# Experts of ten of thirteen tiles run on rows sorted by expert, with indirect DMAs, in a decoder layer on one core

## What is computed

```
gates = softmax(einsum('bsh,eh->bse', x, gate_w) + gate_b)      # 8 experts
top_gates, top_idx = lax.top_k(gates, 2)
expert_out = einsum('bsh,eoh->bseo', x, expert_w) + expert_b
selected = take_along_axis(expert_out, top_idx[..., None], axis=2)
return (selected * top_gates[..., None]).sum(axis=2)
```

## Time and profile before

| | |
|---|---|
| median of the runs | 1438.62 us |
| profiled execution, its own time | 1441.02 us |
| its span, first to last instruction | 1439.2 us |
| granted TensorE clock, mean over the span | 0.969 |
| busy: TensorE, DVE, POOL, ACT | 93%, 63%, 48%, 43% |
| DMA, mean | 35 GB/s |
| start of iteration 15, of iteration 16's first work | 1043.5, 1109.5 us |
| experts behind all chunks, until the last tile's matmuls | 1145.5 to 1435.8 us |

### The profile page before, as it was taken

One profiled execution on the slowest core, in us unless ns is written; L12 is line 12 of the kernel. 1 busy time (PEld: TensorE's weight loads), 2 busy tenths in 40 slices (PEclk: granted clock), 3 DMA queues, 4 the chain that ended last, 5 costly groups with the idle time before them and its releaser, 6 DMA issues.

```text
span 1439.2 us, 43985 instructions
## 1 busy us (share of the span) xinstructions
PE 1341.8 (93%) x19700; PEld 856.9 (60%) x19700; DVE 901.2 (63%) x1463; ACT 614.7 (43%) x888; POOL 684.5 (48%) x642
## 2 busy tenths in 40 slices
PE   4689999999999999999999999999956799999999
PEld 4365766667576666757676675767644444444444
DVE  4657777686777768677776867777563443333332
ACT  4236555555655555564555556455534010000000
POOL 1435757666575666657576665757555100000000
PEclk9899999999999999999999999999967699999999
DMA  7011010101101010110101011010201100101002
GB/s 269 1 39 32 9 44 3 45 8 40 38 8 45 2 45 8 39 38 8 45 3 44 8 40 37 10 45 3 82 31 37 54 30 4 35 36 36 8 0 92
DMA packets 27538, 50.37 MB, mean 35 GB/s; under 512 B 1612, under 2 KB 13188, under 8 KB 27356
## 3 DMA queue, kind: packets, MB, share of 16 engines
q1 hardware_dynamic: 27356, 47.62, 10.2%
HBM read 41.06 MB, written 6.55 MB: 33 GB/s over the span
## 4 chain that ended last, share of the span: by engine, by line
PE 85%; DVE 7%; POOL 3%; ACT 2%; issue 1%; DMA 1%; SPq 0%; POOLq 0%; ACTq 0%; DVEq 0%
PE psum L254 58%; PE psum L664 7%; PE psum L753 6%; PE psum L738 4%; DVE c_most L986 2%; PE psum L682 2%; PE psum L641 2%; DVE c_max L991 2%; PE psum L633 1%; DMA arena<-in_L_attn_Wv 1%; PE psum L345 1%; PE psum L366 1%; POOL arena L1157 1%; PE psum L597 1%; PE psum L649 1%
## 5 line engine op out<-in xcount | busy, mean ns | idle before, releaser
L1157 POOL TENSOR_TENSOR arena<-prob,arena 128x1200 f16<-128x1200 f32 x128 | 314.3, 2467 | 188.3 <-ACT arena L847 188.3
L986 DVE TENSOR_REDUCE c_most<-psum 100x4 f32<-100x1444 f32 x128 | 211.5, 1652 | 21.0 <-PE psum L738 18.8
L254 PE MATMUL psum<-w_kv,cT 128*128 128x512 f16 (+1 forms) x864 | 199.7, 379 | 0.5
L254 PE MATMUL psum<-cT,w_kv 128*128 128x361 f16 x1152 | 196.4, 322 | 0.0
L477 DVE SCALAR_TENSOR_TENSOR w_self_all<-psum,g_now,w_self_all 128x512 f32<-128x512 f32 x104 | 77.8, 750 | 168.6 <-PE psum L254 168.6
L838 ACT ACTIVATE prob<-psum 128x1200 f32<-128x1200 f32 x128 | 149.8, 1170 | 70.5 <-PE psum L753 56.6
L847 ACT ACTIVATE arena<-prob 128x1200 f16<-128x1200 f32 x128 | 151.3, 1196 | 1.5
L254 PEld LDWEIGHTS psum<-cT,w_kv 128*128 128x128 f16 x1152 | 106.0, 99 | 65.2 <-issue 4.0
L254 PEld LDWEIGHTS psum<-w_kv,cT 128*128 128x128 f16 (+1 forms) x864 | 83.4, 101 | 90.6 <-DVE c_raw L901 5.1
L954 DVE SCALAR_TENSOR_TENSOR arena<-psum,b_part,arena 128x361 f16<-128x361 f32 x128 | 74.3, 591 | 86.1 <-ACT arena L819 86.1
L829 ACT ACTIVATE cv<-psum 128x512 f16<-128x512 f32 x96 | 57.3, 597 | 163.0 <-PE psum L254 163.0
(11 more groups left out here) (179 smaller groups left out, 2175.6 us busy)
## 6 DMA issues: line engine op xcount, KB each, us to landing
c_raw<-in_ctx SPq DMA_DIRECT2D x16, 960.0 KB
cT<-in_L_ffn_expert_w SPq DMA_DIRECT2D x4, 1024.0 KB, 5.2
cv<-in_L_ffn_expert_w SPq DMA_DIRECT2D x4, 1024.0 KB, 5.3
x_in<-in_x SPq DMA_DIRECT2D x16, 200.0 KB
x_scratch<-x_out SPq DMA_DIRECT2D x16, 200.0 KB
w_self_all<-x_scratch SPq DMA_DIRECT2D x12, 256.0 KB, 4.4
out<-w_self_all SPq DMA_DIRECT2D x12, 256.0 KB, 2.0
c_raw<-in_ctx SPq DMA_DIRECT2D x16, 123.0 KB
```

Of the source, the lines that this page charges most:

```text
L254: last = pe.matmul(out_ap, a(pa), b(pb), start=(i == 0 and j == 0), stop=(i == len(pairs) - 1 and j == 2))
L986: dve.tensor_reduce(c_most[:, hf], score[0:L, :, 0:HC], AXIS.X, ALU.max).then_inc(max_done, 1)
L1157: pool.tensor_tensor(prob16[o % 2][:, (2 + part) * PT:(3 + part) * PT], prob[:, part], prob16[o % 2][:, part * PT:(part + 1) * PT], ALU.su ...
```

## The change

- The weights of all eight experts are turned in iteration 15, two chunks FW per step from step 5 on (the last two in iteration 16), into one tensor `wT_all` that lies over the weights of attention. SP loads the raw weights of expert e + 2 as soon as expert e is turned.
- The ten early tiles keep a buffer each, and their norm is made in place. Logits get a chunk for each tile.
- Routing of the ten tiles moves to iteration 15, step 15. A new chunk FR computes, for every row, its place among the rows of its expert (11 small matmuls with a triangle and with ones), and DVE derives two slots for every row and the expert of each of 27 slot tiles (`dve_place`, 19 operations with the copy that releases the bank).
- POOL scatters the normed rows into `xs_dram`, 27 x 128 slots, with 20 indirect DMAs (10 tiles, 2 picks) in iteration 16. The slots were set to zero in iteration 1 by a DMA of 27 x 256 KB.
- The experts' stage: 6 dense tiles (experts 0 and 1 on the last three), 27 slot tiles, 18 dense tiles (experts 2 to 7 on the last three), 51 tiles for 104. A slot tile is loaded, turned in fp32, split, multiplied with the weights of the expert whose number TensorE reads into a register, evicted by ACT and stored to `ys_dram`. None is computed ahead of the gate `ALL_CHUNKS`.
- POOL gathers for each row its two results (20 indirect DMAs, four buffers), DVE adds bias, residual and the two parts times their gates, beside the last dense tiles.

```diff
-ROUTE_STEP = 14
+ROUTE_STEP = 15
+SLOT_TILES = 2 * EARLY + E - 1
+SLOTS = SLOT_TILES * P
+DENSE_FIRST = 2
 EXTRA_CHUNKS = {
-    B - 1: {4: ["FX0"], 5: ["FG0", "FW0", "FX1"], 6: ["FW1", "FX2"], 7: ["FW2", "FW3", "FX3"],
-            **{t + 4: [f"FX{t}"] for t in range(4, EARLY)}, LAST_STEP: ["FL0"]},
+    B - 1: {h: ([f"FG0"] if h == 2 else []) + ([f"FX{h - 4}"] if 0 <= h - 4 < EARLY else []) +
+            ([f"FL{h - 5}"] if 0 <= h - 5 < EARLY else []) + (["FR"] if h == ROUTE_STEP + 1 else []) +
+            [f"FW{i // KD}{i % KD}" for i in (2 * h - 10, 2 * h - 9) if 0 <= i] for h in range(2, LAST_STEP + 1)},
...
+        ORDER = ([("dense", e, t) for e in range(DENSE_FIRST) for t in range(EARLY, TT)] +
+                 [("slots", j, None) for j in range(SLOT_TILES)] +
+                 [("dense", e, t) for e in range(DENSE_FIRST, E) for t in range(EARLY, TT)])
+        AHEAD = 2
...
         def ffn_sync(sp):
             sp.wait_ge(chunk_out, ALL_CHUNKS)
+            sp.wait_ge(scattered, 16 * 2 * EARLY)
+            for j in range(4):
+                load_slots(sp, j)
+            for j in range(SLOT_TILES):
+                sp.wait_ge(slot_out, j + 1)
+                sp.dma_start(ys_dram[j * P:(j + 1) * P], slots_out[:, j % 4]).then_inc(slots_stored[j % 4], 16)
+                if j + 4 < SLOT_TILES:
+                    sp.wait_ge(slotsT_low, j + 1)
+                    load_slots(sp, j + 4)
...
+            for i, (kind, a, t) in enumerate(ORDER):
+                if turned_at(i) is not None:
+                    turn_slots(turned_at(i))
+                if i >= 4:
+                    if ORDER[i - 4][0] == "dense":
+                        pe.wait_ge(y_done, dense_count(i - 4))
+                    else:
+                        pe.wait_ge(slot_out, ORDER[i - 4][1] + 1)
...
+                    pe.wait_ge(slotsT_low, a + 1)
+                    e = pe.value_load(expert_i[0:1, a:a + 1], min_val=0, max_val=E - 1)
+                    split3(pe, bank_out, [(lambda p, k=k: slotsT[a % 3][:, p, k],
+                                           lambda p, k=k: wT_all[:, bass.ds(e, 1), k, p].rearrange("p e f -> p (e f)"))
+                                          for k in range(KD)]).then_inc(slot_ready, 1)
...
+        def pool_scatter(pool, t):
+
+            if t == 0:
+                pool.wait_ge(placed, 1)
+                pool.wait_ge(slots_zeroed, 16)
+            for i in range(2):
+                pool.indirect_dma_start(xs_dram[:, :], bass.IndirectOffsetOnAxis(ap=slot_i[:, i, t:t + 1], axis=0),
+                                        y_norm[t], None).then_inc(scattered, 16)
+
+        def ffn_pool(pool):
+            for i in range(4):
+                pool.wait_ge(slots_stored[i], 16 * ((SLOT_TILES - i + 3) // 4))
+            pool.wait_ge(chunk_out, ALL_CHUNKS)
+            for t in range(EARLY):
+                if t >= 4:
+                    pool.wait_ge(sum_done, t - 3)
+                for i in range(2):
+                    pool.indirect_dma_start(part[i][:, t % 4], None, ys_dram[:, :],
+                                            bass.IndirectOffsetOnAxis(ap=slot_i[:, i, t:t + 1], axis=0))\
+                        .then_inc(parts_loaded[t], 16)
...
         def ffn_norm(pool, it, t):
...
-            if t >= 2:
-                before = it if f"FX{t - 2}" in it.order else its[B - 1]
-                pool.wait_ge(chunk_out, before.done(f"FX{t - 2}"))
+            if t >= EARLY + 2:
+                pool.wait_ge(chunk_out, it.done(f"FX{t - 2}"))
...
                 if n == B and h == LAST_STEP:
+                    for t in range(EARLY):
+                        pool_scatter(pool, t)
                     for t in range(EARLY, TT):
                         ffn_norm(pool, it, t)
```

More of the change, by code:

```diff
@@ new lines, in build_layer, with dense_count, turned_at, bias_at @@
+        AHEAD = 2
+        PLACE_CONSTS = 8
+        def dense_count(i):
+            return sum(o[0] == "dense" for o in ORDER[:i + 1])
+        def turned_at(i):
+            return ORDER[i + AHEAD][1] if i + AHEAD < len(ORDER) and ORDER[i + AHEAD][0] == "slots" else None
+        GATES_AT = DENSE_FIRST * LATE + 4
+        BIAS_FROM = len(ORDER) - (E - DENSE_FIRST) * LATE
+        BIAS_ORDER = tuple(range(EARLY, TT)) + tuple(range(EARLY))
+        def bias_at(i):
+            n = i - BIAS_FROM
+            return n if 0 <= n < TT else None
@@ L321, in ffn_sync, with store_sum, load_slots @@
+        def store_sum(sp, t):
+            sp.wait_ge(sum_done, t + 1)
+            sp.dma_start(out.rearrange("b l d -> (b l) d")[t * P:(t + 1) * P], part_sum[:, t % 4])\
+              .then_inc(sum_stored[t % 4], 16)
+        def load_slots(sp, j):
+            sp.dma_start(slots[:, j % 4], xs_dram[j * P:(j + 1) * P]).then_inc(slots_loaded[j % 4], 16)
         def ffn_sync(sp):
             sp.wait_ge(chunk_out, ALL_CHUNKS)
-            def next_raw(e, odd, pair, more):
-                if isinstance(e, int) and e == 0:
-                    load_expert(sp, 2, 0)
-                elif not isinstance(e, int) or e < E - 2:
-                    sp.wait_ge(e_low, KD * e)
-                    load_expert(sp, e + 2, odd)
@@ L330, in ffn_sync @@
-            experts(sp, next_raw)
-            for t in range(TT):
-                n = min(P, T - t * P)
-                sp.wait_ge(y_done, TT * (E - 1) + t + 1)
-                sp.dma_start(out.rearrange("b l d -> (b l) d")[t * P:t * P + n], y[0:n, t]).then_inc(y_stored, 16)
-            sp.wait_ge(y_stored, 16 * TT)
-        def pe_expert_T(pe, e, odd, pair, k):
-            c = KD * (e - 1) + k
-            if k == 0:
-                pe.wait_ge(e_loaded[odd], 16 * (pair + 1))
-            if not (isinstance(c, int) and c < 2):
-                pe.wait_ge(e_low, c - 1)
-            for o in range(KD):
-                last = pe.transpose(psum[:, 4 + k % 2, o * P:(o + 1) * P], raw_e[odd][:, o, k * P:(k + 1) * P], ident[:])
-            last.then_inc(e_T, 1)
@@ L545, in sync_iteration @@
                 sp.dma_start(x2_dram[n - 1], x_out[:]).then_inc(x2_stored, 16)
[L546 to L550 removed]
+            if n == B:
+                for t in range(EARLY, TT):
+                    load_y(sp, t)
             if n < B - 2:
@@ L760, in pe_iteration @@
             for h, step in enumerate(it.steps):
-                if it.n == B and h == LAST_STEP:
-                    pe.wait_ge(chunk_out, it.all_before())
-                    for t in range(AHEAD):
-                        pe_tile(pe, 0, 0, t)
                 for name in step:
@@ L965, in dve_chunk @@
             elif kind == "FL":
[L966 to L970 removed]
+                op = dve.scalar_tensor_tensor(gates[:, i], f[:, 0:E], 1.0 / WSCALE, g_bias[:], ALU.mult, ALU.add)
+            elif kind == "FR":
+                dve_place(dve, f[:, 0:(EARLY + 1) * E].rearrange("p (t e) -> p t e", e=E))
+                dve.wait_ge(placed, 1)
+                op = dve.tensor_copy(best[:, 0:1], slot_f[:, 0, 0:1])
             elif kind == "CV":
```

448 lines of the change are left out of this document (289 added, 159 removed).

## The result

The median is 1364.28 us (1362.64 to 1367.44, four runs) against 1437.17 us of the kernel before on the same chip (1434.79 to 1440.55, four runs): a ratio of 0.9489 [0.9466, 0.9511], 5.1% faster. The forecast was 1345 (1311 to 1385): the direction is right, the time lies inside the range, and the forecast is 19 us too low. The profiled execution took 1362.64 us with a span of 1360.9. The changed kernel was timed once more beside later experiments: 1367.23 us, ratio 0.9503 [0.9481, 0.9524]. The brackets behind a ratio are its 95% interval.

What follows compares the result with a forecast made beforehand. TensorE, busy 93% of the span, bounds the kernel, except iteration 15 (a DVE, ACT and POOL chain). Of 149 us saved, 11 go for early tiles, 17 gate, 12 turning slots, 19 late loads, the rest in transitions: 1345 us (1311 to 1385).

Steps and rivals of the forecast that it cites:

- rival that ends slower: Scatters and gathers: POOL held through each indirect DMA, reaching 1439 at 4.2 us each, about 1469 at 5.0; chance 4%.
- Slots: 27 slot tiles: late loads make 3.77 us per tile, 3.85 with the register load; 100.7 us for the tiles.
- The second rival: Slot tiles: the register load drains TensorE, 15 to 33 us more, 1360 to 1378; chance 14%.
- Half clock in the slots: Slot tiles: waits of 0.8 us per tile keep TensorE at 1.2 GHz, 164 us for 101, time 1408; chance 8%.
- Scatter: POOL in iteration 16: 20 indirect DMAs at 1.2 us, 24 us in all, ahead of the norms of tiles 10 to 12.
- Iteration 15, net +8: Iteration 15 gets 8 us longer from turning weights, routing and placement, less POOL's waits; bounds -11 to +31.
- Routing and placement, 4.5 + 2.5: Iteration 15: routing adds 4.5 us to the chain, placement, behind PV1's 2.8 us of matmuls, 2.5.
- The chunks FW, 9.5: Iteration 15: about half of 19.3 us of evictions for 26 more chunks and the logits is not covered, 9.5 us.
- POOL's waits, -8.5: Iteration 15: POOL no longer waits for FX chunks before reusing two y_norm buffers, which gives 8.5 us back.
- Zeroing, "nothing": Iteration 1: zeroing 27 x 256 KB beside some 60 us of matmuls, on DMA engines 15% busy, costs nothing.
- Dense tiles with biases: End of the experts' stage: 18 tiles at 2.59 and 13 biases at 0.96 take 59.1 us.
- Gate: Before the experts: norms and logits keep their 10 us and the experts' gate opens at 1162.5, 17 us later.

Runs made afterwards that it cites:

- Experiment 1: Changed kernel with SP loading slot tile j + 4 before it waits for tile j's result and stores it: 1345.33 us, ratio 0.9367.
- Experiment 7: Experiment 1 with a fixed expert's weights for each slot tile, no register load or arithmetic: 1344.94 us, ratio 0.9344.
- the four profiles: Profiles of the changed kernel (twice), Experiment 1 and Experiment 7, identical up to the slots; 124.17 to 128.69 us from batch 13's store to batch 15's.
- Experiment 5: Changed kernel with routing at step 17 and chunk FR at step 18 of iteration 15, not 15 and 16: 1358.13 us, ratio 0.9442.
- Experiment 6: Changed kernel with 16 of 32 chunks FW, experts 4 to 7 using the weights of 0 to 3: 1351.26 us, ratio 0.9388.
- experiment 8: Changed kernel with the old wait put back, POOL's norm of tile t waiting for chunk FX of tile t - 2: 1368.54 us, ratio 0.9514.
- experiment 2: Changed kernel with SP issuing expert 4's load before it waits for and stores batch 14 in iteration 15: 1362.03 us, ratio 0.9477.
- experiment 3: Changed kernel with slots zeroed by nine DMAs in iterations 1 to 9, not one in iteration 1: 1357.27 us, ratio 0.9459.

## Why the prediction came out as it did

**The direction and the main saving: right.** 53 tiles fewer against some 37 us given back in waits is what the page shows, and no rival that ends slower came near: an indirect DMA held POOL for 1.27 us, not 4.2.

**Slots: right in the total and in the loop, with luck in the terms.** The forecast had 3.77 us per tile from a loop over two tiles, 3.85 with the register; the trace has 3.76. The forecast's lap was 4.5 us from one tile's matmuls to the next turning and 3.03 of turning and matmuls. The trace has 3.9 and 3.63 (7.52 together): the load landed sooner than taken, and behind each wait the turning, the gap and the matmuls take 0.6 us more. The two misses cancel, which is luck. Experiment 1 takes 18.7 us off the stage, where the sum had 19 for late loads. Of the register load the forecast said that it is hidden unless TensorE waits for a load, and took 0.08 per tile. Experiment 7 against experiment 1 shows both halves: nothing where TensorE runs on, 0.41 us behind a wait. In the changed kernel 0.20 of gap and 0.17 on the matmuls in each lap are near 0.19 per tile. The second rival, 1 to 2 us in every tile, falls. The Trainium skill's floor of about 600 ns for a register load ("DMA: Bandwidth & Descriptors", "Latency and other measured facts") does not hold here: the trace has 0.30 us for the median of 27 such loads and 0.55 for the longest.

**Half clock in the slots: wrong as a rival.** The granted clock was 0.50 before the gate and rose in the first tiles behind it (12.31 us for four, against 10.36 in the earlier trace rows). From 1188 us on it was 1.00, though 14 us of waits are spread over the slots.

**Scatter: right, in size partly by luck.** 1.27 us each for 1.2; 1.6 us more over the twenty. POOL is not held until the data land, as the forecast took it, but the rows only bounded the price between 0.43 and 2.7, and 1.2 was a choice between them. **Gather: right.** 0.95 us on POOL plus 0.30 (median landings 4.0 and 4.4), and DVE never waited for the rows; on the contrary POOL waited for DVE to free the buffers.

**Iteration 15, net +8: the step that was off, by 2.4 to 6.9 us** in the four profiles (+10.4 to +14.9; the table's profile has the most). Four of its terms were mis-sized or missing.

- Routing and placement, 4.5 + 2.5. They stand on the chain whole, 7.9 + 4.5 us. Placement was to hide behind PV1's 2.8 us of matmuls; that overlap was not there, since PV1's matmuls started only behind placement's last copy, after a wait of 4.00 us. Routing was to take 5.7 us, less 1.2 hidden; nothing of it was hidden, and one of its small operations took 2.37 us in place of 0.24 (last section). Experiment 5 gets 4 to 7 us back by moving routing.
- The chunks FW, 9.5 for half of their evictions and the logits'. On the chain of the four profiles the evictions on ACT and DVE have 7 to 8 us, so that half was about right. The turnings on TensorE, 11 to 24 us more in the forecast's own count, were given no term in the net sum, and 6 to 10 us of them are on the chain. Experiment 6 prices a whole chunk at 0.52 to 0.64 us, 14 to 17 for the 26.
- POOL's waits, -8.5. Before, the chain of iteration 15 does pass through POOL (12.4 of its 66 us), and in the changed kernel through none of it, so the waits were rightly read as a path. What they were worth was not: put back alone they cost 1 to 4 us (experiment 8), since other work is nearly as late behind them.
- The expert's load behind SP's wait for batch 14 was missing from the sum, about 2 us (experiment 2).

These single prices add to more than was measured, so they overlap: relief in one place is partly taken by the next. How they share the difference stays open.

**Zeroing, "nothing": wrong.** It was costed against the DMA engines' mean idle share; a transfer that fills them for 21.5 us still cost 3.5 us at batch 13 of the profiled run (4.8 to 6.7 in the three like it), 6.5 at the norms by experiment 3. That is about as large a miss as that of iteration 15.

**Dense tiles with biases: 2.6 us short.** 18 x 2.59 + 13 x 0.96 was priced from rows where four bias passes run together. Alternating, the chain has 1.05 for a bias and 2.70 for the tile, 0.20 more per pair, 13 x 0.20 = 2.6.

**Gate: +1.2 us**, the norms and logits took 11.4 where 10.2 were kept. No run varied this. In the traces TensorE, which the tiles computed ahead kept busy before, is at 0.50 there (0.83 before), and a turning on the chain takes 1.10 and 0.97 us (0.64 and 0.87 before).

## What to carry to other kernels

On a queue that executes in order, put the transfer whose data have long been ready ahead of the one that waits for the last result: here that order alone was worth 19 us. A wait that an edit removes is worth only the lead that it has over the next path, so put it back alone before you believe in the gain. Give work that is added to a stage with a dependency chain a term for each engine that it visits, the matmuls too, and before you hide it behind other work ask whether an engine in order starts that work first. Split a transfer of megabytes over several iterations.

## What was not expected of the hardware

An indirect DMA of 128 rows of 2 KB holds POOL for 0.96 us and 0.30 more until the next one starts, 1.27 in all (1.25 for a gather), while its data land 2.7 to 4.4 us after it is issued (medians by group): POOL does not wait for the data.

One DMA of 6.9 MB cost TensorE gaps of 2.46 and 0.66 us in which nothing was awaited, and the kernel about 4.6 us by the store of batch 0; in nine pieces it cost nothing that shows there.

One small DVE operation took ten times its usual time beside a large one on POOL (timeline of the changed kernel, iteration 15):

```profile
1107.78 2.55 POOL L1336 TENSOR_TENSOR bank<-prob,bank 128x1200 f16<-128x1200 f32 x1 [2.06 <-ACT bank L1019]
1108.05 2.37 DVE L539 TENSOR_TENSOR route_all<-route_all,rank 128x80 f32<-128x80 f32 x1
...
1111.83 0.24 DVE L539 TENSOR_TENSOR route_all<-route_all,rank 128x80 f32<-128x80 f32 x1
```

All ten profiles with routing at step 15 have it (2.37 or 2.38 us), and it ends within 0.2 us of POOL's operation. With routing at step 17 (experiment 5) L539 takes its 0.24 us, and another small operation, which takes 0.24 in the changed kernel, is caught in its place:

```profile
1118.82 2.46 POOL L1336 TENSOR_TENSOR bank<-prob,bank 128x1200 f16<-128x1200 f32 x1 [11.75 <-ACT bank L1019]
1118.92 2.47 DVE L579 TENSOR_TENSOR of_pick<-route_all,slot_of 128x80 f32<-128x80 f32 x1
```

So the slowness goes with the neighbour and not with the operation: both operations have two operands in SBUF, start just behind POOL's and end with it. It costs 2.1 us on the chain of iteration 15.
